# Late weights made ready in the head by GpSimd, and the last 14 groups' fp16 halves shared by three engines, in a decoder kernel

## What is computed

```python
x = layernorm(x + self_attention(x, Wq, Wk, Wv, Wo))
# cross-attention: no batch boundary in the softmax over 16 * 375 context rows
sim = einsum('hid,hjd->hij', q, k) * SCALE
sim = (sim - mean(sim)) * 1.5 + mean(sim)
x = layernorm(x + einsum('bni,iq->bnq', softmax(sim) @ v, Wout) + bout)
# feed-forward: both weights are made ternary (-1, 0, 1) around half their mean magnitude
h = gelu(einsum('bsd,fd->bsf', x, ternary(W1)) + b1)
x = layernorm(x + einsum('bsf,df->bsd', h, ternary(W2)) + b2)
```

## Time and profile before

| | us |
|---|---|
| three runs, lowest, median, highest | 2422.36, 2422.67, 2423.64 |
| the profiled execution, its own time | 2421.85 |
| span of its records | 2420.1 |
| TensorE matmuls busy (share of the span) | 2297.3 (95%) |
| VectorE busy | 2050.3 (85%) |
| ScalarE busy | 1866.5 (77%) |
| GpSimd busy | 1836.5 (76%) |

### The profile page before, as it was taken

One profiled execution on the slowest core, in us unless ns is written; L12 is line 12 of the kernel. 1 busy time (PEld: TensorE's weight loads), 2 busy tenths in 40 slices (PEclk: granted clock), 3 DMA queues, 4 the chain that ended last, 5 costly groups with the idle time before them and its releaser, 6 DMA issues. The chain is left out here.

```text
span 2420.1 us, 67977 instructions
## 1 busy us (share of the span) xinstructions
PE 2297.3 (95%) x28874; PEld 2049.5 (85%) x28874; DVE 2050.3 (85%) x2250; ACT 1866.5 (77%) x2178; POOL 1836.5 (76%) x1097
## 2 busy tenths in 40 slices
PE   7998999999999999999989999999999999998687
PEld 4557998899889988999889988998899989997574
DVE  7778888888888888888878888888888888889777
ACT  4447887888878888888878888888888888888235
POOL 8314887888878887888778887888788978999301
PEclk9999999999999999999999999999999999999899
DMA  6201000000000000000000000000000000202211
GB/s 200 74 1 32 7 4 12 6 4 6 13 4 6 4 13 6 4 6 13 4 7 4 6 13 4 6 7 10 6 7 4 7 4 6 60 7 52 64 47 30
DMA packets 33765, 46.61 MB, mean 19 GB/s; under 512 B 2272, under 2 KB 27328, under 8 KB 33472
## 3 DMA queue, kind: packets, MB, share of 16 engines
q1 hardware_dynamic: 33472, 42.35, 6.1%
HBM read 28.91 MB, written 13.43 MB: 17 GB/s over the span
## 5 line engine op out<-in xcount | busy, mean ns | idle before, releaser
L1176 POOL TENSOR_TENSOR e_lo<-ring,e_hi 128x1024 f16<-128x1024 f32 (+1 forms) x672 | 1400.4, 2102 | 174.4 <-ACT ring L694 147.5
L837 DVE TENSOR_TENSOR run_max<-psum,run_max 128x1024 f16<-128x1024 f32 (+1 forms) x616 | 738.8, 1199 | 267.0 <-ACT ring L679 266.7
L679 ACT ACTIVATE ring<-psum 128x1024 f32<-128x1024 f32 (+1 forms) x672 | 674.7, 1004 | 230.7 <-PE psum L388 147.3
L858 DVE SCALAR_TENSOR_TENSOR ring<-ring,psum 128x1024 f32<-128x1024 f32 (+1 forms) x672 | 795.0, 1188 | 9.5 <-PE psum L610 9.4
L407 PE MATMUL psum<-v_main,e_hi 128*128 128x129 f16 x4032 | 720.1, 220 | 10.2 <-POOL e_lo L1176 10.2
L388 PE MATMUL psum<-qx_hi,k_hi 128*128 128x256 f16 x2632 | 718.3, 273 | 7.4 <-DVE run_max L837 7.3
L409 PE MATMUL psum<-v_main,e_hi 128*128 128x128 f16 x4032 | 720.5, 222 | 0.0
L388 PE MATMUL psum<-qx_lo,k_hi 128*128 128x256 f16 x2632 | 718.2, 273 | 2.4 <-issue 2.4
L411 PE MATMUL psum<-v_main,e_lo 128*128 128x129 f16 x4032 | 718.5, 219 | 0.0
L388 PE MATMUL psum<-qx_hi,k_lo 128*128 128x256 f16 x2632 | 718.2, 273 | 0.0
L694 ACT ACTIVATE ring<-ring 128x1024 f32<-128x1024 f32 (+1 forms) x672 | 695.5, 1035 | 3.5 <-DVE ring L858 2.8
(11 more groups left out here) (189 smaller groups left out, 2816.1 us busy)
## 6 DMA issues: line engine op xcount, KB each, us to landing
o_scratch<-o_buf SPq DMA_DIRECT2D x56, 129.0 KB, 2.7
raw<-o_scratch SPq DMA_DIRECT2D x16, 451.5 KB, 3.8
stage<-in_ctxT SPq DMA_DIRECT2D x6, 500.0 KB, 4.0
stage<-in_ctxT SPq DMA_DIRECT2D x12, 250.0 KB, 4.9
w_scratch<-wall SPq DMA_DIRECT2D x1, 2304.0 KB, 11.0
wall<-w_scratch SPq DMA_DIRECT2D x6, 384.0 KB, 3.9
x<-in_xT SPq DMA_DIRECT2D x4, 448.0 KB, 6.1
res<-in_x SPq DMA_DIRECT2D x1, 1792.0 KB, 14.7
```

The source lines that it names most:

```text
L679: a.activation(ring[:, f % SLOTS, 0:n], pair(f)[:, 0:n], ACT.Copy).then_inc(s_kept, 1)
L837: ins = v.tensor_tensor(run_max[:, 0:n], pair(f)[:, 0:n], run_max[:, 0:n], ALU.max)
L858: v.scalar_tensor_tensor(slot, slot, LIFT, psum[:, 6, 0:QB].unsqueeze(1).broadcast_to([P, t, QB]), ALU.add, ALU.subtract).then_inc(s_sub, 1)
L1176: g.tensor_tensor(e_lo[f % NEL][:, 0:n], slot, e_hi[f % NEH][:, 0:n], ALU.subtract).then_inc(s_lo, 1)
```

## The change

- **The weights of the last stages are made in the head.** Behind the last context load, SP loads Wout and W1T into the two staging buffers, and W2T over the part of `wall` that has been saved. GpSimd scales and splits Wout, waits for the thresholds, and makes the ternary weights in six whole passes of 2,048 columns: for each of W1T and W2T "greater than", "less than", and their difference. SP saves the four results to DRAM (`t_scratch`). In the last head SP fetches these fp16 tiles where it fetched the fp32 weights.
- **The sums and thresholds move with them**: VectorE's sums for W1T behind round 6, for W2T behind round 8, four each; TensorE's matmul with `ones` at the end of round 8; the thresholds behind round 9.
- **The norms move** from rounds 8, 9, 10, 11, 13, 14 to rounds 10 to 15, since GpSimd's additions of `bout` stand behind the ternary passes; the statistics from rounds 7, 9, 12 to 9, 11, 13, and the first two blocks of queries from rounds 10, 11 to 12, 13.
- **The last 14 groups**, f from 658 on: ScalarE makes `e_hi` of all of them, VectorE `e_lo` of the odd ones (`low_weights`, two groups ahead of `attend`), GpSimd `e_lo` of the even ones only. The sums, Wout's split, thresholds and ternary steps are gone from there.
- **The output stage's loads** are written out one by one, each with a wait for the stores it needs in place of a wait for all.

The core of the diff:

```diff
-        NORMS = {8: (0, 1), 9: (2, 3), 10: (4, 5), 11: (6, 7), 13: (8, 9), 14: (10, 11)}
-        STATS = {7: 0, 9: 1, 12: 2}
+        NORMS = {10: (0, 1), 11: (2, 3), 12: (4, 5), 13: (6, 7), 14: (8, 9), 15: (10, 11)}
+        STATS = {9: 0, 11: 1, 13: 2}
...
+        SUMS = {6: 0, 8: 1}
+        LATE, LOW_AHEAD = NF_ALL - 14, 2
...
                 def attend(f, more, more_sides):
-                    pe.wait_ge(s_lo, more + (f + 1))
+                    if f < LATE:
+                        pe.wait_ge(s_lo, more + (f + 1))
+                    elif f % 2:
+                        pe.wait_ge(s_lo_odd, (f - LATE) // 2 + 1)
+                    else:
+                        pe.wait_ge(s_lo, LATE + (f - LATE) // 2 + 1)
...
+                        if b == 8:
+                            pe.wait_ge(s_abs, 9)
+                            pe.matmul(psum[:, 6, 0:8], lhsT=ones[:, :], rhs=sum_p[:, :],
+                                      start=True, stop=True).then_inc(s_total, 1)
...
@@ scalar
-                    if weights % 2 == 0 and 0 <= weights < NF_ALL:
+                    if (weights % 2 == 0 or weights >= LATE) and 0 <= weights < NF_ALL:
                         exp_half(weights)
...
@@ vector
+                def low_weights(f):
+                    n = cols_of(f % NGRP)
+                    v.wait_ge(s_exp, f + 1)
+                    v.wait_ge(s_av, f - NEL + 1)
+                    v.tensor_tensor(e_lo[f % NEL][:, 0:n], ring[:, f % SLOTS, 0:n], e_hi[f % NEH][:, 0:n],
+                                    ALU.subtract).then_inc(s_lo_odd, 1)
...
+                def weight_sums(i):
+                    v.wait_ge((s_w1, s_w2)[i], 16)
+                    for x in range(4):
+                        v.tensor_reduce(sum_p[:, 4 * i + x:4 * i + x + 1], (w1_32, w2_32)[i][:, x * WP:(x + 1) * WP],
+                                        AX.X, ALU.add, apply_absolute_value=True).then_inc(s_abs, 1)
...
+                        if b in SUMS:
+                            weight_sums(SUMS[b])
+                        if b == 9:
+                            thresholds()
...
+                    if LATE <= f + LOW_AHEAD < NF_ALL and (f + LOW_AHEAD) % 2:
+                        low_weights(f + LOW_AHEAD)
...
@@ gpsimd
+                g.wait_ge(s_wout, 16)
+                g.wait_ge(s_wsave, 16)
+                run(g.tensor_scalar(wout32, wout32, WSCALE, 1.0, ALU.mult, ALU.mult))
+                run(g.tensor_copy(wsplit[:, 0, :], wout32))
+                g.tensor_tensor(wsplit[:, 1, :], wout32, wsplit[:, 0, :], ALU.subtract).then_inc(s_wl, 1)
+                g.wait_ge(s_wl, 1)
+                g.wait_ge(s_t, 4)
+                for i, (w32, temp) in enumerate(((w1_32, t12[:, 1, :]), (w2_32[:, :], below[:, :]))):
+                    run(g.tensor_scalar(t12[:, i, :], w32, above_of[:, i:i + 1], None, ALU.is_gt))
+                    run(g.tensor_scalar(temp, w32, below_of[:, i:i + 1], None, ALU.is_lt))
+                    g.tensor_tensor(t12[:, i, :], t12[:, i, :], temp, ALU.subtract).then_inc(s_tern, 1)
+                    g.wait_ge(s_tern, i + 1)
                 g.wait_ge(s_bias, 32)
...
+                    if f >= LATE and f % 2:
+                        continue
...
@@ sync, the head
+                sp.wait_ge(s_staged, len(tasks) - 1)
+                sp.dma_start(stage[1]..., Wout...).then_inc(s_wout, 16)
+                sp.wait_ge(s_staged, len(tasks))
+                sp.dma_start(stage[0]..., W1T...).then_inc(s_w1, 16)
+                sp.wait_ge(s_wsave, 16)
+                sp.dma_start(w2_32..., W2T...).then_inc(s_w2, 16)
+                sp.wait_ge(s_wl, 1)
+                sp.dma_start(t_dram[2:4]..., wsplit[:, :, :]).then_inc(s_tsave, 16)
+                sp.wait_ge(s_tern, 2)
+                sp.dma_start(t_dram[0:2]..., t12[:, :, :]).then_inc(s_tsave, 16)
                 sp.wait_ge(l_cp, NB)
```

More of the change, by code:

```diff
@@ L231, in build @@
         ones48 = at(FOLD + 1216, "ones48", [T, 3 * DH_S], F32)
+        w1_32 = stage[0][:, :, :].rearrange("p k n -> p (k n)")
+        wout32 = stage[1][:, :, :].rearrange("p k n -> p (k n)")
+        wsplit = at(VREG2, "wsplit", [P, 2, W12], F16)
+        w2_32 = at(VREG2 + 8192, "w2_32", [P, W12], F32)
+        t12 = at(VREG + 8192, "t12", [P, 2, W12], F16)
+        below = at(VREG, "below", [P, W12], F16)
+        ones = at(EREG + 15584, "ones", [P, P], F32)
+        sum_p = at(FOLD + 1408, "sum_p", [P, 8], F32)
+        scale, above_of, below_of = [at(FOLD + 1440 + 32 * i, n, [P, 2], F32)
+                                     for i, n in enumerate(("scale", "above_of", "below_of"))]
+        s_w1, s_w2, s_wout = sem("a_w1"), sem("a_w2"), sem("a_wout")
+        s_abs, s_total, s_t, s_tern, s_wl = sem("a_abs"), sem("a_total"), sem("a_t"), sem("a_ternary"), sem("a_wout_lo")
+        s_tsave = sem("a_late_saved")
+        SUMS = {6: 0, 8: 1}
         assert VREG + 23552 <= QREG and RING + 12 * NTP * 2 <= RING + 43392 and NTP * 24 <= 43392
@@ L657, in _ @@
                     blocks(2 * NQB, 4 * NQB, pairs * 2)
-                blocks((NH - 2) * NQB, NBLK - 1)
-                for s in range(NGRP):
-                    step(NBLK - 1, s)
-                    if s == 6:
-                        pe.wait_ge(s_free, side_number(NBLK, 0))
-                        pe.wait_ge(s_abs, 9)
-                        pe.matmul(psum[:, 7, 0:8], lhsT=ones[:, :], rhs=sum_p[:, :],
-                                  start=True, stop=True).then_inc(s_side, 1)
+                blocks((NH - 2) * NQB, NBLK)
             @block.scalar
@@ L793, in _ @@
                 self_attention()
+                a.wait_ge(s_tsave, 32)
                 number = 0
@@ L1093, in _ @@
                             norm(LATE_NORMS[f + LEAD] + 2)
-                    if n == NBLK - 2 and s == 7:
-                        v.memset(ones[:, :], 1.0).then_inc(s_abs, 1)
-                    if n == NBLK - 2 and s >= 8:
-                        weight_sum(s - 8)
-                    if n == NBLK - 1:
-                        if s < 4:
-                            weight_sum(4 + s)
-                            low_wout(s)
-                        elif s == 6:
-                            v.wait_ge(s_side, number + 1)
-                            thresholds(psum[:, 7, 0:8].rearrange("p (w x) -> p w x", w=2))
-                        elif s in (8, 9, 10, 11):
-                            ternary(2 * s - 16)
-                            ternary(2 * s - 15)
             @block.gpsimd
```

106 lines of the change are left out of this document (43 added, 63 removed).

## The result

The changed kernel takes 2432.59 us (median of 7 runs, 2431.64 to 2436.23) where the kernel before, measured beside it, takes 2423.64: a ratio of 1.004 with a 95% interval from 1.0028 to 1.0052. It is slower, by some 9 us, and lies outside the predicted range of 2412.5 to 2427.5. The profiled executions stand 11.9 us apart in span (2432.0 and 2420.1), some 3 more than the medians of the runs, so that a sum over the two traces is known no better than that.

The account below looks back on a forecast made before the run. TensorE was taken to bound the head and most of the loop, GpSimd then VectorE the loop's end. Terms -16.1 + 0.7 + 4.2 + 6.0 + 2.0 = -3.2 us gave 2419.5 us, range 2412.5 to 2427.5.

Parts of the forecast that it names:

- The norms: Head, rounds 10 on: GpSimd's six ternary passes take 16.5 us and delay norm 2; +6.0 us.
- Rival A: Head: comparisons are dear on GpSimd, 4.22 us each in place of 1.90; +6.1 us in sum, 2428.8; chance 0.10.
- The two-input passes: Head: GpSimd's two subtractions of ternary tiles, taken at 4.22 us each from two `e_lo`.
- B's first part: Head: GpSimd's subtraction of two 16-bit tiles takes 1.90 us for 4.22, -4.6; clearly-faster rival, chance 0.34.
- B's second part: Head: TensorE's clock stays up, -2.0 us; with the faster subtraction -9.8, 2412.9; clearly-faster rival, chance 0.34.
- The stall of round 8: Head: TensorE's matmul with `ones` waits for VectorE's sums ahead of round 9; +4.2 us, plus 1.5 of clock.
- The sums behind round 6: Head: four VectorE reductions of 2.4 us, mostly swallowed by slack before TensorE wants the next maximum; +0.7 us.
- Wout's split: Head: GpSimd's scaling and splitting of Wout (1.90 + 1.90 + 4.22) lies in its 25.81 us idle gap; cost zero.
- The predicted head of 12.9: Head: the added costs +0.7, +4.2, +6.0 and +2.0 us, putting GpSimd's first `e_lo` near 224 us.
- The clock: Head: TensorE's clock drops after pauses of round 8 (1.5) and rounds 10 and 11 (0.5); +2.0 us.
- The tail: Loop's end: ScalarE sets the pace at 2.09 us per group, `o_buf` 10.5 earlier, output stage starts sooner; -16.1 us.
- Rival C: Loop's end: VectorE's `e_lo` waits for the port shared with GpSimd, 7 us lost, net +4, 2426.7; chance 0.08.

Follow-up runs that it names:

- the probes: Three edits of the changed kernel, other operations in place of GpSimd's four comparisons, each run once for its profile: 2435.29, 2419.48 and 2430.21 us.
- the head alone: The changed kernel with the last 14 groups put back to their old division of the exponentials: 2443.70 us, ratio 1.0086.

## Why the prediction was wrong

**The step that failed** is in *The norms*: "GpSimd then has four one-input passes over 2048 columns, 1.90 each by its scaling of `stage`". They take 5.44. The scaling was taken as the nearest row because it has one input and as many elements; it has two operations, and the probes show that among one-input passes the operations, and whether there are one or two, set GpSimd's pace. The six passes then took 30.4 us in place of 16.5, on the path of norm 2, which waited 8.61 us for them. Four times 3.54 is 14.2 us, and with the passes made as fast as priced the time fell by 14.7. Rival A had named this mechanism and its place. It got a chance of 0.10 and an end of 4.22, the two-input row, that was too low: its condition, 3.9 us per comparison, was met. With 5.44 and the same working the sum is -3.2 + 14.2 = +11.0, so 2433.7, 1.1 from the result (2.0 from the measured change of 9.0). That is near by luck in part: round 9 is missing from it on one side, the fifth block and the output stage (below) on the other. The bound from both sides failed because its ends were a row with two operations and one with two inputs, and neither had a single operation. The Trainium skill (GPSIMD Engine Reference, Performance pitfalls for Q7 kernels) has bodies that compare at 2.03 cycles an element, and at 1.03 when unrolled by two; the trace shows 2.9 times the scaling's time for the comparison, and nearly the same for a single multiplication, which compares nothing, so it was the right warning for another reason.

**The two-input passes** took 4.05 on two fp16 tiles, not 1.90: the forecast's 4.22 held, and B's first part did not. B's second part didn't either, the clock fell.

**The stall of round 8** was right to 0.01 us (5.71 for 4.2 + 1.5), and the kernel without it was 4.4 faster, since round 7 gets longer by the sums. The 0.01 is luck: by windows of 1 us, TensorE was at its lower level for some 6.8 us from 113 on, twice the 3.4 that the clock's 1.5 was taken from, and a part of that cost stands in round 9. The sums behind round 6 were right (0.64 for 0.7), and Wout's split was hidden as told.

**Round 9 and the hold of `rstd`** were missing. I had put the hold by the port at `rows` only; an instruction on four elements waited 5.34 us as well, with TensorE already at half its clock (0.50 from 115 to 120 us). Round 9 was 5.43 longer. About 2.1 of this came before the hold: `rstd` was issued 8.97 us into the round (126.41), where it stands 6.90 into round 7 in the kernel before (102.38). In the run with the priced passes the round was 10.62 long, so 3.5 of this were a term of the head even then. The predicted head of 12.9 nonetheless comes out there, at 13.6, by luck: the norms cost 3.8 there and not 6.5, and by VectorE's holds, not by the wait of norm 2 for `res` that they were priced by.

**The clock** was priced at 2.0. It showed 0.73 on average from 115 to 160 us, with TensorE busy for 26.66 of 45. I can't part its cost from the waits that bring it down.

**The tail** was right in its steps: 2.10 us per group for 2.09, `o_buf` 10.4 nearer for 10.5, `rden_c` 1.53 behind it, -16.2 in all for -16.1. Its split was not: the prediction has the ternary work's going worth "some 6" alone, and by the trace of the head alone it was worth 8.7, with 2.9 of it ahead of `o_buf`. Rival C did not come: VectorE's `e_lo` took 1.22 to 1.23, only the last, of 768 columns, 1.32 where another took 0.95, and ScalarE had no gap.

**Not in the sum** were the loop's fifth block (-3.3), present in all 14 kernels with the new head, and absent from the two with the old one, and 1.5 less in the output stage.

**Of the signs** named for being wrong, two came: the first `e_lo` after 230, and comparisons over 3 us.

## What to carry to other kernels

A row prices an instruction only if it has the same operations, not just the same engine, shape and number of inputs; where no row has them, an upper end drawn from other operations is no bound, and the chance of a dear case on a naked path should be larger than 0.10. On GpSimd, write one-input elementwise passes as pairs that have been measured fast, and put long passes directly behind the work that another engine waits for, short enough to end before that engine wants the shared port. Where two engines bind a stage in a row, as at this loop's end, price each edit with the other in place: the division brought 2.4 us alone and some 7.5 behind the other edit.

## What the hardware showed unexpectedly

- GpSimd's `tensor_scalar` over 128 x 2,048 fp32 takes 1.89 to 2.00 us with times-times, times-plus, plus-times or smaller-larger, 5.37 to 5.45 with a single operation (times, greater or less), and 7.09 to 7.17 with greater-times, plus-smaller, larger-times or times-larger. A pointer for the scalar costs 0.08, and an fp16 or fp32 result makes no difference.
- A VectorE instruction on 112 x 4 elements was held for 5.34 us, and two `rows` for up to 11.48, by GpSimd's passes; VectorE's reductions, reciprocals and operations with an input in PSUM beside them were not.
- The blocks of the loop repeat from kernel to kernel within some 0.3 us, all but two. One of these is 3.3 us shorter in all kernels with the new head, and in the changed kernel VectorE's two held steps in it are 1.9 us shorter. That it hangs on how VectorE and GpSimd stand to one another when the loop starts is argued, not tested.
